# Macaron block on one core: context steps in groups of four, weights awaited one by one, two input buffers, a new order of work

## What is computed

```python
def ffn(X):                                   # per sample
    shared = silu(X @ sW1 + sb1) @ sW2 + sb2
    act = sqrt(softplus(X @ routing_W.T + expert_bias))
    combine = top-2 of act, one-hot times value          # [tokens, 8]
    hdn = silu(X @ rW1[e] + rb1[e]); y = hdn @ rW2[e] + rb2[e]
    return shared + sum_e combine[:, e] * y[e]
def attn(x):
    q, k, v = split_heads(x @ Wq), split_heads(x @ Wk), split_heads(x @ Wv)
    scores = q . k over a window of 64 (self and the 63 before) / 4
    return (softmax(scores) @ v) @ Wo
x = x + 0.5 * ffn(layernorm(x))       # pass p
x = x + attn(layernorm(x))            # attention
x = x + 0.5 * ffn(layernorm(x))       # pass q
```

## Time and profile before

| | us |
|---|---|
| median of 3 runs | 1632.12 (1631.79 to 1634.74) |
| the profiled execution | 1630.6 |
| its span, first to last instruction | 1628.5 |
| PE busy | 1504.9 (92%) |
| DVE busy | 1203.6 (74%) |
| ACT busy | 1118.3 (69%) |
| POOL busy | 816.9 (50%) |

### The profile page before, as it was taken

The page is one execution under the profiler, slowest core; times in us unless marked ns, Lnnn a source line. Parts: engine busy times, 40 slices in busy tenths (PEclk is TensorE's granted clock), DMA queues, the critical chain, the costliest instruction groups (busy, mean ns, idle before and its releaser), DMA issues.

```text
span 1628.5 us, 40855 instructions
## 1 busy us (share of the span) xinstructions
PE 1504.9 (92%) x13632; PEld 1330.6 (82%) x13632; DVE 1203.6 (74%) x4771; ACT 1118.3 (69%) x3400; POOL 816.9 (50%) x789
## 2 busy tenths in 40 slices
PE   0867999999999999999999999999999999999876
PEld 0656788889888888988888898888888888889665
DVE  4455787887878788687878878787887878786644
ACT  2346777777767767786766777776777777677643
POOL 1325464555556465465546555554555555464433
PEclk9989999999999999999999999999999999999888
DMA  3135453635454353535436363544526353454401
GB/s 99 53 109 145 121 153 96 165 118 150 122 141 141 99 155 115 160 121 150 131 99 161 101 167 127 145 124 115 158 88 181 118 145 117 132 144 120 138 17 65
DMA packets 270052, 203.86 MB, mean 125 GB/s; under 512 B 154474, under 2 KB 224516, under 8 KB 269844
## 3 DMA queue, kind: packets, MB, share of 16 engines
q1 hardware_dynamic: 266352, 201.14, 43.5%
q10 hardware_dynamic: 3460, 0.04, 0.1%
q0 software_dynamic: 32, 0.07, 0.0%
...
## 4 chain that ended last, share of the span: by engine, by line
PE 57%; DVE 22%; issue 8%; ACT 5%; POOL 5%; DMA 2%; SPq 2%; DVEq 0%; ACTq 0%; POOLq 0%
PE gb L759 9%; PE gb L761 8%; PE gb L760 8%; PE yb L759 6%; PE yb L761 6%; PE yb L760 6%; PE ptb L818 4%; PE sb_ L809 3%; PE cxb L836 3%; DVE pr L642 3%; DVE xn L589 2%; POOL pr L379 2%; ACT xn L472 2%; POOL sq L390 2%; DVE xl L667 1%
## 5 line engine op out<-in xcount | busy, mean ns | idle before, releaser
L396 POOL TENSOR_TENSOR gl<-ag,gh 128x512 fp32r<-128x512 f32 x288 | 382.5, 1333 | 218.8 <-ACT gh L498 218.6
L379 POOL TENSOR_TENSOR pr<-pr,rinv 128x512 f32<-128x512 f32 x256 | 300.8, 1175 | 345.0 <-DVE rinv L650 341.5
L453 ACT ACTIVATE pr<-pr,mx 128x128 f32<-128x128 f32 x1024 | 397.0, 395 | 41.5 <-DVE mx L642 41.5
L759 PE MATMUL yb<-w2h,gh 128*128 128x256 f32 x1152 | 335.2, 291 | 5.5 <-POOL gl L396 5.4
L760 PE MATMUL yb<-w2h,gl 128*128 128x256 f32 x1152 | 321.8, 279 | 0.0
L761 PE MATMUL yb<-w2l,gh 128*128 128x256 f32 x1152 | 321.5, 279 | 0.0
L642 DVE CUSTOM_DVE_ANT_0 pr<-sb_,mask 128x128 f32<-128x128 f32 x1024 | 235.8, 285 | 97.8 <-issue 94.8
L498 ACT ACTIVATE gh<-ag 128x512 fp32r<-128x512 f32 x288 | 179.4, 627 | 126.8 <-DVE ag L711 86.4
L759 PE MATMUL gb<-xh,w1h 128*128 128x512 f32 x576 | 247.8, 430 | 9.2 <-DVE qkl L622 7.9
L504 ACT ACTIVATE tt<-gb,b1half 128x512 f32<-128x512 f32 x288 | 195.9, 680 | 83.0 <-PE gb L761 81.2
L711 DVE SCALAR_TENSOR_TENSOR ag<-tt,ag 128x512 f32<-128x512 f32 x288 | 233.5, 815 | 2.6
...
## 6 DMA issues: line engine op xcount, KB each, us to landing
gate<-gates_pair SPq DMA_DIRECT2D x256, 256.0 KB, 3.7
ks<-qk_dram SPq DMA_DIRECT2D x256, 128.0 KB, 2.9
qs<-qk_dram SPq DMA_DIRECT2D x512, 64.0 KB, 2.5
...
```

Source lines behind the costliest of these rows:

```text
L379: nc.gpsimd.tensor_tensor(pr[:, k], pr[:, k], rinv[:, k, :].unsqueeze(2).to_broadcast([P, NP, P]), ALU.mult).then_inc(a_pn, 1)
L396: nc.gpsimd.tensor_tensor(gl[:, k, :], ag[:, k, :], gh[:, k, :].bitcast(F32), ALU.subtract).then_inc(f_gl, 1)
L453: nc.scalar.activation(pr[:, k, r, :], pr[:, k, r, :], ACT.Exp, bias=mx[:, k, r:r + 1], scale=-1.0, accum_out=rsum[:, k, r:r + 1]).then_in ...
L759: nc.tensor.matmul(dst, ah, bh, start=start, stop=False, **kw)
```

## The change

Four things change.

- **Order.** One list per engine (`ORDER`) is kept for the middle; the first samples (`HEAD`) and the last ones (`TAIL`) have lists of their own with sample numbers in them. The middle list is a new one too.
- **Context in groups.** Four `U` steps become one (`UG` = 4), issued as U3, U7, U11 and U15; `pt` has six buffers instead of two (`NPT`).
- **Two inputs.** `xin` has two buffers (`NXI`), so x[b+1] doesn't wait for T of pass p of sample b. Attention's normalized rows have a tensor of their own, `axn`, instead of sharing `xn`.
- **Weights apart.** Seven groups of weights have a semaphore each; their high and low parts (`Wh..`, `Wl..`) are steps in the lists of ACT and DVE, and PE waits for a group at its first use. The raw expert weights land in `va` instead of a tensor of their own, rW1 in two DMAs instead of eight; the two memsets of `qs` and `va` are a step `Wz` behind most of those splits; the bias rows are loaded by SP instead of ACT.

```diff
-        NG, NTT, NPR, NPT, NBANK = 2, 2, 2, 2, 3
-        YB2 = 4
+        NG, NTT, NPR, NPT, NBANK, NXI, NX1, LEAD = 2, 2, 2, 6, 3, 2, 2, 2
+        YB2, UG = 4, 4
...
+        axn = sb("axn", [P, NT, D])
...
-        raw = sb("raw", [P, E * KC * P])
-        b2f = tt[:, 0, 0:D]
+        b2f = pt[:, 0, 0:D]
+        raw = va[:, :, :, :].rearrange("p h b d -> p (h b d)")
...
                 if s == "LX":
-                    if b > 0:
-                        sp.wait_ge(f_res, 2 * nth("p", b - 1) + 2)
-                        sp.dma_start(xin, x[b].rearrange("(t p) d -> p t d", p=P)).then_inc(x_in, 16)
+                    if b >= NXI:
+                        sp.wait_ge(f_res, 2 * nth("p", b - NXI) + 2)
+                    sp.dma_start(xin[b % NXI], x[b].rearrange("(t p) d -> p t d", p=P)).then_inc(x_in[b % NXI], 16)
...
                     if m == 0:
                         sp.wait_ge(f_g1, 16 * n + 16)
+                        if n == 0:
+                            sp.wait_ge(w_lo, lo_done("2r"))
...
-            act.wait_ge(w_raw, 16 * (E + 7))
-            for dst, src in splits(w1h, w2h, wah):
-                nc.scalar.activation(dst, src, ACT.Copy).then_inc(w_hi, 1)
...
+                    else:
+                        dst, src = split(k, w1h, w2h, wah)
+                        act.wait_ge(w_in[WK.index(k)], 16 if k in ("1s", "2s", "2r") else 32)
+                        nc.scalar.activation(dst, src, ACT.Copy).then_inc(w_hi, 1)
...
-            pe.wait_ge(w_lo, NSPLIT + 2)
-            pe.wait_ge(w_prep, 6)
-            pe.wait_ge(w_zero, 5)
...
                 elif s[0] == "U":
...
-                    for hd in range(2):
-                        for r in range(NP):
-                            mm = nc.tensor.matmul(cxb[32 * r:32 * r + 32, w, :],
...
+                    for w in range(j % NW - UG + 1, j % NW + 1):
+                        k = (NJ * b + c * NW + w) % NPT
+                        v, blk, _ = value_of(w)
+                        for hd in range(2):
+                            for r in range(NP):
+                                mm = nc.tensor.matmul(cxb[32 * r:32 * r + 32, w, :],
...
+                        mm.then_inc(a_pv, 1)
```

The middle of the new lists, as far as the prediction speaks of it (offsets are relative, as before):

```diff
+    "PE": """
...
+qX0-6 qX1-6 pY5-4 pH8-4 P6-5 pY6-4 qL-6 S9-5 P7-5 qH0-6 P8-5 U7-5 S10-5 pY7-4 pY8-4 S11-5 P9-5 qC-6 P10-5
+S12-5 qH1-6 qH2-6 P11-5 S13-5 aX0-4 qY0-6 S14-5 aX1-4 U11-5 qH3-6 qH4-6 Q00-4 qY1-6 Q01-4 V0-4 P12-5 qH5-6
...
+    "DVE": """
...
+ri6-5 pa7-4 pg7-4 ri7-5 qxl0-6 qxl1-6 mx8-5 pa8-4 pg8-4 ri8-5 qLr-6 mx9-5 qLq-6 qR1-6 ri9-5 ctl0-5 mx10-5
+pT-4 qR2-6 ri10-5 aN1-4 mx11-5 qa0-6 qg0-6 mx12-5 ri11-5 mx13-5 qa1-6 qa2-6 qg1-6 ri12-5 qg2-6 axl0-4 ri13-5
```

More of the change, by code:

```diff
@@ L724, in step @@
                             ALU.mult, ALU.add).then_inc(f_res, 1)
-            run(ORDER_DVE, step)
+            run("DVE", step)
         @block.tensor
@@ L878, in step @@
                     k = (NE * n + e) % NG
+                    weights("2s" if e == 0 else "2r", n == 0 and e < 2)
                     pe.wait_ge(f_gl, NE * n + e + 1)
```

454 lines of the change are left out of this document (321 added, 133 removed).

## The result

The changed kernel takes **1714.9 us** (median of 4 runs, 1711.9 to 1717.1) against 1632.0 for the kernel before on the same chip: ratio 1.0504, 95% interval 1.0484 to 1.0524, so 5% slower where 3% faster was forecast. Its profiled execution has a span of 1715.4 us (before 1628.5).

The account below looks back on a forecast made before the run. PE was taken to bound the kernel, with the middle's gain given back at the router's chain. S0 of sample 2 at 234 + 12 x 94.1 + drain 219.5 = 1582.7, plus 2.3 gives 1585 us; range 1540 to 1622.

Parts of the forecast that it names:

- S0 of sample 2: First scores step of sample 2, end of start and fill: about 234 us instead of 281.3, bounds 222 and 255.
- twelve middle samples: Middle of the kernel: 94.1 us per sample against 93.9 now, so the twelve take 1129 us as before.
- drain: Last stretch, 218.6 us before, keeps its work: 219.5 us, bounds 208 and 228.
- Work of PE, 88.4 per sample: PE's steps in a sample without waits: 88.4 us instead of 91.5, since context groups save 3.1 net.
- In the rest of the list I find the partner done before PE comes: Middle list outside the router: PE finds its inputs ready, with one exception of 0.2 us (P11).
- The router's place, 5.2: Around P10 and S12 of pass q: PE waits 4.3 us plus 0.9 for DVE and POOL, giving back the groups' gain.
- one chain from L: DVE and POOL steps from L to P10 in pass q: 12.7 to 13.9 us, or 11.5, against 8.4 of PE.
- The lower clock: Rival: router waits in the middle lower PE's clock, a sample takes 98.2 us and the total 1634; chance 0.10.
- my own signs: Middle: PEclk 1.00 expected, under 0.95 means the clock rival, which decides from 98.3 us per sample on.
- the start gives less: Rival: DVE's splits and memsets or load order hold PE, S0 of sample 2 at 255, total 1606; weaker start or groups 0.17.
- "Slower": Whole kernel slower than before: chance 0.09; its rival was waits in the middle costing PE's clock, total 1634.
- The faster middle: Rival: router chain overestimated, PE waits 2.7 us, a sample takes 91.2, total 35 us less, 1550; chance 0.25.

Follow-up runs that it names:

- both together: OUT and mask 6 early (1647.4), router of pass q cut to one instruction each for ranks and softplus, mask 10 ahead of reciprocal 9, residual of pass p behind mask 11: 1621.9 us.
- filling the wait: Changed kernel with PE computing pH6 of samples 3 to 14 four times over, same result, where PE waits for mask 6: 1696.7 us.

## Why the prediction was wrong, step by step

The forecast was 1585; the changed kernel takes 130 us more. By the terms of its sum:

| term | forecast | measured | difference |
|---|---|---|---|
| S0 of sample 2 | 234 | 254.6 | +20.6 |
| twelve middle samples | 1129 | 1224.3 | +95 |
| drain | 219.5 | 236.5 | +17 |
| beyond the span | 2.3 | -0.5 | -2.8 |

- **Work of PE, 88.4 per sample: right** (88.45). The spacings as the prediction prints them add up to 91.0 and not to 91.5 before the change; the walk gives 91.5. The group gain of 3.1 and the count of runs hold. The Trainium skill has a rule that would account for it (TensorEngine Tiling (Array Packing), section Key Properties): changing the tiling mode drains TensorE. The runs agree: with ten changes of shape fewer per sample (14 runs to 4) PE's work fell by 3.1 us; they don't separate the drain from the rest of a step's edges.
- **"In the rest of the list I find the partner done before PE comes": the step that failed.** The sum has 0.5 us for all of it (0.3 for pass p, 0.2 for P11). I compared PE with DVE, ACT and POOL, and SP's list not at all. OUT stood behind ST10 there, in plain sight; the trace of before had the price of such twelve issues (8 us), and even the wait of aR for the store, 5.9 us in the whole program. In its place the runs show 7.4 us per sample, 5.2 of waiting for the store and 2.2 of the lower clock behind it, 60 to 67 us of the total.
- **The router's place, 5.2: nearly right in size, half right in cause.** Measured 6.9: the five steps come 4.8 late (3.2 by the brackets), and 2.1 are the lower clock, which the sum has at nothing. The instruction times added up well: R1 took 1.85 us, since POOL was idle as I had said (forecast 1.8). The port rule that I drew on from the Trainium skill (SBUF — State Buffer, section SBUF: two separate sides) so gave the right side. What I took for one chain from L is two of about equal length, and the second starts at PE's own pY8. Shortening the router alone gave 0.2 us; both together 2.9.
- **The lower clock: a rival at 0.10 that came true in part.** I had it decide from 98.3 us per sample and only in place B. By my own signs it would have been taken for the cause (102.0 us per sample, PEclk 0.94, where I had named 98.3 and 0.95), and it isn't the larger part. It costs 2.2 us at place A (measured by filling the wait); at place B the surplus of S12, qH1 and qH2, 2.1 us, is of the same kind by the granted clock there (0.50). It is a consequence of the waits: with both chains and the late store gone PEclk is 1.00.
- **Start.** First matmul 21.9 (forecast 15): the first DVE step waits for b1's slow loads, which share a semaphore with the router's bias; taken apart, it comes at 16.0, close to the forecast, and S0 of sample 2 still at 248.2 and not 234. So S0 of sample 2, 254.6, met the number of the rival "the start gives less" (255), and b1's loads are 6 us of the 20.6; S0 of sample 0 was already 12.5 late (112.5, forecast 100). And S0 of sample 2 was the wrong milestone: the new order gets there with 18.7 us less of PE's work done, 6.5 of which are the groups. Measured by idle time the start and fill gain nothing.
- **Drain, +17.** I kept it as it was. The last lists carry place B too (S0 of sample 14 to 15 takes 95.1 us instead of 87.2), attention of sample 15, from S0 to O0, takes 6.4 us more, and from L to C of the last pass 15.4 us instead of 11.6.
- **The rivals.** None gave 1715. "Slower" was priced at one mechanism of 4 us per sample and had a chance of 0.09; the range ended at 1622, since I took a list in which I found the partner done "before PE comes" as read. The faster middle didn't come.
